# The second mixture's batches: taken up three tiles behind their last tile, their outputs loaded from SyncE's queue instead of ScalarE's

## The reference

```python
x = x + 0.5 * ffn0(layernorm(x))      # mixture of 8 experts, top 2, 128 -> 512 -> 128, tanh gelu
x = x + attention(layernorm(x))       # 16 heads of 8, rotary, softmax
x = x + 0.5 * ffn0(layernorm(x))      # the same 8 experts again: "the second mixture"
x = x + 0.5 * ffn1(layernorm(x))      # 16 experts, top 2, capacity 640 rows each, exact gelu
x = x + linear_attention(layernorm(x))
x = x + 0.5 * ffn1(layernorm(x))
```

## Time and profile before

| | |
|---|---|
| time, three runs | 1413.46, 1418.72, 1420.01 us (median 1418.72) |
| the profiled execution | time 1414.94 us, span 1412.8 us |
| busy, share of the span | PE 1172.9 us (83%), DVE 850.4 (60%), ACT 733.3 (52%), POOL 701.8 (50%) |
| chain that ended last, by engine | PE 56%, DVE 18%, POOL 7%, DMA 6%, issue 6%, ACT 5% |
| HBM traffic | 157 GB/s over the span |
| the second mixture's tiles | about 710 to 885 us |
| the sends behind its last tile | 890.6 to 938.3 us |

### The profile page before, as it was taken

The page is one execution under the profiler, slowest core; times in us unless marked ns, Lnnn a source line. Parts: engine busy times, 40 slices in busy tenths (PEclk is TensorE's granted clock), DMA queues, the critical chain, the costliest instruction groups (busy, mean ns, idle before and its releaser), DMA issues.

```text
span 1412.8 us, 25297 instructions
## 1 busy us (share of the span) xinstructions
PE 1172.9 (83%) x7427; PEld 780.9 (55%) x7427; DVE 850.4 (60%) x2809; ACT 733.3 (52%) x1579; POOL 701.8 (50%) x940
## 2 busy tenths in 40 slices
PE   4399897899999999999689998239999777399994
PEld 3299885222223232232278988128799565278893
DVE  7534666889889999988432666702116786421234
ACT  4155543577767767767544554213445566233441
POOL 3777443213233454524754477744554377635553
PEclk9999998799999999999879999559999888589997
DMA  9687767435435435241357876425577301145586
GB/s 304 176 223 218 206 188 228 150 102 159 146 92 159 134 82 147 68 145 36 120 143 230 259 235 187 135 77 169 163 216 239 126 31 45 47 150 172 179 259 191
DMA packets 171543, 223.71 MB, mean 158 GB/s; under 512 B 24001, under 2 KB 125889, under 8 KB 171409
## 3 DMA queue, kind: packets, MB, share of 16 engines
q1 hardware_dynamic: 133168, 174.67, 42.5%
q0 software_dynamic: 18080, 37.20, 7.7%
q10 hardware_dynamic: 20160, 10.23, 2.5%
HBM read 150.55 MB, written 71.21 MB: 157 GB/s over the span
## 4 chain that ended last, share of the span: by engine, by line
PE 56%; DVE 18%; POOL 7%; DMA 6%; issue 6%; ACT 5%; SPq 2%; DVEq 1%; ACTq 0%; POOLq 0%
PE PS L1508 17%; PE PS L1518 17%; DVE arena L2434 5%; PE PS L1696 5%; PE PS L1672 5%; POOL dispatched L830 5%; PE PS L1486 3%; ACT arena L1223 2%; PE PS L1680 2%; PE PS L1658 2%; DVE X L1981 2%; DMA arena<-experts 2%; DVE BST L1971 1%; DMA qk_products<-arena 1%; DVE arena L2083 1%
## 5 line engine op out<-in xcount | busy, mean ns | idle before, releaser
L1094 ACT ACTIVATE arena<-PS,arena 128x128 f32<-128x128 f32 (+2 forms) x696 | 280.4, 451 | 347.6 <-PE PS L1508 333.2
L852 POOL DMA_INDIRECT expert_out<-arena x309 | 298.2, 965 | 291.0 <-issue 174.6
L1223 ACT ACTIVATE arena<-PS 128x512 f32<-128x512 f32 x512 | 284.0, 597 | 134.9 <-PE PS L1672 133.9
L2434 DVE TENSOR_REDUCE arena<-PS 128x2 f32<-128x1024 f32 x256 | 300.9, 1217 | 26.7 <-PE PS L1682 25.8
L1508 PE MATMUL PS<-arena 128*128 128x128 f32 (+2 forms) x1392 | 310.0, 366 | 5.4 <-DMA arena<-experts 1.9
L1518 PE MATMUL PS<-arena 128*128 128x128 f32 (+1 forms) x2472 | 306.2, 275 | 4.0 <-DVE arena L2243 3.5
L1518 PEld LDWEIGHTS PS<-arena 128*128 128x128 f32 x2472 | 297.7, 192 | 17.7 <-issue 6.1
L2243 DVE TENSOR_TENSOR arena<-PS,arena 128x128 f32<-128x128 f32 (+2 forms) x174 | 68.7, 395 | 326.6 <-PE PS L1518 324.4
L1508 PEld LDWEIGHTS PS<-arena 128*128 128x128 f32 x1392 | 222.3, 195 | 47.5 <-issue 7.9
L830 POOL DMA_INDIRECT dispatched<-arena x192 | 185.2, 965 | 80.7 <-issue 55.3
L1672 PE MATMUL PS<-arena 96*128 96x512 bf16 x512 | 174.1, 391 | 11.8 <-ACT arena L1223 5.4
(11 more groups left out here) (273 smaller groups left out, 1180.9 us busy)
## 6 DMA issues: line engine op xcount, KB each, us to landing
arena<-experts SPq DMA_DIRECT2D x103, 578.0 KB
qk_products<-arena SPq DMA_DIRECT2D x48, 384.0 KB
arena<-qk_products SPq DMA_DIRECT2D x64, 288.0 KB
arena<-experts SPq DMA_DIRECT2D x71, 256.0 KB
dispatched<-FILL SPq DMA_DIRECT2D x32, 322.5 KB, 2.6
YC<-expert_out SPq DMA_DIRECT2D x36, 256.0 KB
arena<-dispatched SPq DMA_DIRECT2D x71, 129.0 KB
arena<-qk_products SPq DMA_DIRECT2D x64, 128.0 KB, 5.0
```

Of the source, the lines that this page charges most:

```text
L852: pool.indirect_dma_start(YK, bass.IndirectOffsetOnAxis(ap=ID[:, s:s + 1], axis=0), YS[:, s, :], None).then_inc(s_yo[r], 16)
L1094: act.activation(bent(f, tau)[:, q, 0:N], bank(q, 0, N), func, bias=bias).then_inc(s_g, 1)
L1223: act.activation(PT[:, G % 2, j, k, :], bank(4 + k % 2), ACT.Exp, scale=float(1.0 / np.sqrt(HD))).then_inc(s_exp, 1)
L2434: dve.tensor_reduce(MX[:, G % 2, head:4:2, a], PS[:, 1024 * w:1024 * w + 1024].rearrange("p (a b) -> p a b", a=2), AX_X, ALU.max).then_inc ...
```

## The change

Two numbers of `start_of` are lowered, so that batches 0 to 5 of the second mixture start one step earlier (16, 18, 22, 26, 30, 34 instead of 17, 19, 23, 27, 31, 35); batches 6 and 7 stay at 40 and 42. The two loads of each of these six batches leave ACT's program for SP's, where they stand behind the weights of tile s and ahead of the rows and weights asked for next. Which tiles a load waits for is unchanged.

```diff
@@ start_of
             if carries(L):
-                return max(tiles_to(L, b) + 4, early_tiles(L) + E0 + 3 + 2 * b)
+                return max(tiles_to(L, b) + 3, early_tiles(L) + E0 + 2 + 2 * b)
@@ SyncE, moe(L)
                     rows_in(tau + XRING - RING)
                     expert_in(tau)
+                    for b in early_starting(L, tau) if carries(L) else []:
+                        outputs_landed(f, outputs_of(L, b))
+                        fetch(L, b)
@@ ScalarE, moe(L)
                     if c < tiles:
                         gelus(c)
-                    for b in early_starting(L, c + 2) if carries(L) else []:
-                        wait_outputs(act, f, outputs_of(L, b))
-                        load_outputs(act, L, b)
```

## The result

| | before | after |
|---|---|---|
| median of 22 runs each | 1417.49 us (1413.46 to 1420.26) | 1422.01 us (1413.84 to 1426.16) |
| ratio, 95% interval | | 1.0026 [1.0015, 1.0038] |
| profiled execution | time 1414.94, span 1412.8 | time 1417.83, span 1416.0 |
| busy PE, DVE, ACT, POOL | 1172.9, 850.4, 733.3, 701.8 | 1177.2, 850.9, 735.1, 702.7 |
| last send issued | 937.35 | 941.45 |

The account below looks back on a forecast made before the run. The prediction took POOL's unbroken queue of scatters and sends to bound the end, PE's pace its start. An earlier start (-1.19 us) and SP's loads (+1.35) gave +0.2 us; it forecast 1417.0 us, range 1412 to 1424.

Parts of the forecast that it names:

- The 18.50 us from hidden(20) to the copy of tile 22: PE and DVE ahead of POOL's run: this stretch moves unchanged to hidden(19) through the copy of tile 21.
- The chain of the hold: Batch 0 on SP: scatter of tile 12 lands, two issues, rows, late weights 17; PE stalls 1.69 us at hidden(17).
- no second stall at hidden(19): Batch 1: weights 19 land at 792.09, PE arrives at 792.08, so no further stall.
- DVE's cover: Gather of batch 0 delays the copy of tile 15 some 1 us, covered by the late hidden(17).
- the load of weights: Weights in SP's queue behind YC: 5.36 us taken; 4.80 to 7.4 us considered.
- the loop: Batches 3 to 5, SP waiting for POOL, DVE, PE, weights: 15.4 us against POOL's 19.05, costing 0 until loads take 9.0.
- rival 3: SP's hold feeds on itself through far longer weights loads: at 12 us, +15.8 us, 1430.7; chance 0.09.
- Rival 2: ACT's waits were the bound: PE gains their 7.1 us and 1.2 more, 1406.6; chance 0.04.
- the sum: Whole kernel: -1.19 us for the earlier start, +1.35 for loads on SP, together +0.2 us.
- such a scatter takes 2.31 us to land: SP's wait for a scatter ahead of batch 0's loads: landing at 776.47 after issue at 774.16.
- PE will stall at tiles 31 and 35, inside its slack: Later batches: PE's weight stalls stay within its 2.6 us to spare at the last tile, leaving no gap on POOL.
- Rival 4: In between: loads of 7.4 to 9.8 us, or PE's 2.6 us not sufficing in the tail; +2 to +7, chance 0.13.

Follow-up runs that it names:

- sp_only: Against the kernel before: SP issues the loads of batches 0 to 5, starts stay as before; 1415.3 us, ratio 0.9988, -1.7 us.
- change_weights_first: The change with weights asked for ahead of rows in SP's loop of the second mixture; 1.0015 against the kernel before, +2.1 us.
- fetch_later: The change with SP waiting and loading one loop step later, new starts kept; 1.0020 against the kernel before, +2.8 us.
- two_early: The change with only batches 0 and 1 starting earlier, 2 to 5 at the old starts; 1.0004 against the kernel before, +0.6 us.
- sp_hold: sp_only with each load waiting for one scatter more, that of tile s - 4; 1422.62 us, 1.0030 against the kernel before, +4.3 us.
- sp_hold_01: sp_only with only batches 0 and 1 waiting for one scatter more; 1423.84 us (5 runs), 1.0046 against the kernel before, +6.5 us.
- sp_hold_25: sp_only with only batches 2 to 5 waiting for one scatter more; 1.0012 against the kernel before, +1.7 us.
- sp_weights_first: sp_only with weights asked for ahead of rows in SP's loop; 0.9991 against the kernel before, -1.3 us.
- four_early: The change with only batches 2 to 5 starting earlier, 0 and 1 at the old starts; 1.0022 against the kernel before, +3.1 us.

## Why the prediction came out as it did

**What held.** The bound: the second mixture ends with POOL's last send, in one run of 1.27 us issues, 100 of them from the scatter of tile 21. The 18.50 us from hidden(20) to the copy of tile 22 moved whole: from hidden(19) at 794.12 that is 812.62, plus 1.17 gives 813.79, the trace to the hundredth. The chain of the hold, its place, no second stall at hidden(19), DVE's cover, the load of weights (5.36 taken, 3.98 to 5.52 seen), and with it that the loop does not run away (rival 3). Rival 2 was wrong in size; sp_only's -1.7 us are the most that could be its. The range of 1412 to 1424 holds 1422.0, and the change is under 0.5% as forecast, but neither is to the credit of the sum: a loss of 4.1 us in the stretch stood against its +0.2, and the range is 12 us wide.

**The term that failed: "such a scatter takes 2.31 us to land".** Where SP waits, it took 4.28, 5.26, 4.36 and 4.92 us. The 2.31 came from one scatter at 856.32. Rows at hand said otherwise of the place itself: the second scatter of tile 12 was issued at 774.16, and ACT, waiting for it, issued its load at 778.39, 4.2 us later; that of tile 14 was issued at 781.63, and ACT's load for batch 1 came 5.5 us later (kernel before):

```profile
787.12 1.04 ACTq L553 DMA_DIRECT2D YC<-expert_out  x2
```

What differs is in the issue times of the change: weights at 774.31, scatter at 774.43. The copy of tile s - 4 releases both, the load into the buffer that it frees and the scatter of what it wrote, so the 64 KB scatter goes out beside 578 KB. No run was made to test this, but the chains of all runs between 740 and 900 us bear on it. The 19 scatters there with a load of weights issued within 0.3 us of them took 3.83 to 5.38 us. The four with none issued from 5 us ahead of them until they landed took 2.24 us each, such as this one of change_weights_first:

```profile
862.92 2.24 DMA expert_out<-arena
```

In between the time isn't decided by that distance alone: with the last weights 1.79 us ahead it was 2.31 (the kernel before, 856.32), with 1.94 us ahead 4.12 (fetch_later, 841.60). The Trainium skill ("DMA: Bandwidth & Descriptors", Anatomy of one DMA) fits 2.0 us plus bytes at 436 GB/s, 2.15 us for 64 KB: the 2.24 and the 2.31 agree, the 4.28 to 5.26 don't.

The head with measured sizes: landing +1.97, the two issues 1.77 instead of 0.93, +0.84, table reads +0.07, load 4.02 instead of 5.36, -1.34, and 0.12 between landing and issue: hidden(17) 1.66 us later than forecast, hidden(19) 3.11 us late instead of 1.35. Two errors of opposite sign hid much of the mistake.

**The step that failed: "PE will stall at tiles 31 and 35, inside its slack".** It stalled at four tiles, 23 and 27 too, and beyond the slack. The loop was closed for POOL's sake ("It isn't starved: 0, until a load takes 9.0 us"), but its price to PE was never summed. With the landing at 4.4 to 5.3 us each batch's hold reaches past the time at which PE wants its weights, and stalls and half clock make tile 38 late by 5.7 us against a slack of 3.7 (the 2.6 of the prediction left out that POOL now has a tile's four issues more before tile 38, 5.1 us, for a start 3.7 us earlier). It is the same term once more, an estimate: less the excess of the landing over 2.31 (2.95 us at batch 2, 2.05 at 3, 2.1 at 4, from 840.51 to SP's issue at 845.09, 2.61 at 5), the stalls of 0.93, 1.94, 2.41 and 0.78 us would leave some 0.3. The clock stayed at the head, for which the prediction had expected it, and that was luck of this execution: in two_early, sp_hold and sp_hold_01 it fell behind the first stall. Of the tail the prediction said nothing, and there it fell. Rival 4 had named this case ("a tail in which PE's 2.6 us don't suffice", +2 to +7) and gave it 0.13; it is what happened.

**Why a tile earlier brought so little.** The gain was small from the start: POOL-bound, 3.73 us of an earlier start pay 2.54 for two more issues in the run. Against a gain of 1.2 us, 2.0 us of gaps and 1.35 + 1.76 = 3.1 us at the head are enough to turn the sign.

**What stays open.** Whether the earlier start gives its 1.2 us at all; how the head's loss splits between stall and clock. Single profiles differ upstream of the change, at the second scatter of tile 12 by -0.8 us (sp_only) to +4.8 (sp_hold_01) against before, and in whether the clock falls, so tenths are read within one trace and verdicts from all runs. From that scatter to the last send it is 163.2 us before, 163.6 in sp_only, 164.0 in sp_hold_25, 167.0 in the change, 167.2 in two_early, 168.2 in sp_hold_01 and 171.3 in sp_hold: the holds are in every one of the slower traces, but two_early's +0.6 us and sp_hold's +4.3 don't match theirs.

The best version is sp_only: the loads on SP, the old starts. It beats the change by 5.4 us. Against the kernel before it gains 1.7 us, barely shown: 0.1 us lies between its interval and no gain, it is the best of twelve variants, and sp_weights_first (-1.3) can't be told from it.

## What to carry to other kernels

A wait on a queue that prefetches holds everything behind it; put it where what it waits for has already landed. One step later was enough for that here, and it was free where nobody needed the data a step earlier (sp_only), not where somebody did (fetch_later, +2.8 us). Take a DMA's latency from the instance that this wait will see, with the traffic that the same event sets off beside it, and not from the fastest row of the same kind. Slack that one engine has on another is a budget: sum every stall charged to it, and the clock that a stall may cost.

## What the runs showed of the hardware

- **One kind of scatter, two latencies.** 128 rows of 512 bytes landed in 2.31 us at 856.32 of the kernel before, and in 4.28 to 5.26 us in the change where a weights load of 578 KB was issued within 0.3 us of it. Over all runs it was 3.83 to 5.38 us in 19 such cases, and 2.24 in four with no such load near.
- **A stall sometimes halves PE's clock.** After idles of 2.41 us (the change, 853.03), 3.38 and 4.55 (sp_hold) and 3.09 (sp_hold_01) the eight matmuls of a hidden layer took 3.63, 3.39, 3.78 and 2.42 us instead of 1.99. So they did, at 3.36 to 3.78 us, after 2.77 (sp_hold_25), 2.87 (four_early), 3.24 (change_weights_first) and 3.98 (two_early). After 3.18 us (the change, 786.55) they took 1.99, as they did after 1.94 (833.21). The granted clock in sp_hold, as a mean over each stretch:

```profile
785.00:793.00 8.00, 4.90 (x37) 4.44 (x35) 4.18 (x16) 1.77 (x4) 2.57 (x3) 1.00 0.74 211
793.00:798.00 5.00, 4.72 (x19) 4.07 (x20) 1.00 (x8) 1.91 (x4) 1.92 (x2) 0.66 0.94 278
```

- **An issue on SP can take longer.** The second of batch 0's two YC issues took 1.35 us in the change (779.25), where such an issue took 0.50 to 0.52 at batches 2, 3 and 5.
